# A third PSUM bank for the visits, two matmul groups in another bank, and the router's steps one place earlier

## The chip, the cores and the metric

The kernel runs on one core of a Trainium2 chip. The metric is the device time of one execution in microseconds. Three timed runs of the kernel before gave 4075.95, 4081.71 and 4083.36 us (median 4081.71). The profiled execution took 4071.0 us.

## What is computed

Two layers over a graph of 6,250 nodes with 256 features and 106,250 edges sorted by destination (self-loops included). The change lies in the second layer alone, which is, for node rows x:

```
xn  = layernorm(x)
x   = x + (xn @ W_self + mean over edges of xn[src] @ W_neigh + b) + mix(xn)
mix(xn): attn = softmax(k^T v) per head over all nodes;  y = xn + attn applied to q
         y + gelu(layernorm(y)*g + b @ w_fc1 + b_fc1) @ w_fc2 + b_fc2
h   = layernorm(x)
x   = x + shared_mlp(h) + sum over the best 2 of 4 experts of weight * expert(h)
      (weights: softmax(h @ gW + gb), top 2, softmax again; MLPs of three layers with relu)
```

All of it is in fp32.

## The kernel before, in words

Nodes stand in 49 tiles of 128 rows. The program is a row of blocks; each ends with all engines meeting. Three of the blocks are passes over the edges, and this change touches the last one (from L1813) and the short block ahead of it (L1702 to L1809).

**The short block** loads the mixer's weights by eight DMAs on SyncE's queue (L1707 to L1714), all counted on one semaphore. TensorE and VectorE then turn the Gram matrix of xn into a 256x512 weight `gws` (attention and W_self folded in), in a chain of small matmuls and copies. Its temporaries (`wqkv`, `gram`, `t1` and so on) lie in `rows`, the ring of 16 buffers that the third pass will gather edge rows into. GpSimd meanwhile sets the whole accumulator `ACC` (12544 columns) to zero (L1719), clears one temporary (L1720) and writes a constant (L1721). TensorE starts after all eight DMAs and all three of these.

**The third pass.** The sorted edges make 880 *visits* of 128 edges each. GpSimd gathers the 128 source rows of a visit into the ring by one indirect DMA (L1847), at most 16 ahead of TensorE. TensorE multiplies them with a 128x128 one-hot matrix (L1940, two instructions per visit), which ScalarE (L1858, L1862) or VectorE (L2044) has made. The product goes to half a PSUM bank, a pair of visits fills a bank, and the banks alternate between `ps[0]` and `ps[1]`: before pair n TensorE waits (L1938) until VectorE has added pair n-2. VectorE adds each half to `ACC` (L2056) once the pair is complete, and it loads the column offsets of 16 visits into registers at every sixteenth visit (L178 is the helper).

Between the visits the rest of the layer is worked off. Function `turns` (L732) writes the order by hand. Turn i has 18 or 19 visits and 18 *places* q = 0 to 17 (and a last one); at each place an engine first issues its `side(i, q)` and then one visit. In turn i the work is on four tiles: na = i+1 (attention product), b = i (the mixer's MLP), s = i-1 (residual and norm, VectorE alone), f = i-2 (experts). Every engine keeps its own program order; only semaphores tie them. What matters here, with TensorE's places first:

- q0, q1, q2: transposes for na, f and b (L1963, L1968, L1973). q3: gate logits (L1978), then the first-layer groups of the experts `first_ffn` k = 0 (L1955). q4: k = 1, 2. q5: k = 3, then a wait for `lg` (VectorE has read the gate logits, L2104), because k = 4 goes to the bank columns where they lay; then k = 4. q6: k = 5. q7: the attention product, 4 instructions of 512 columns into the whole of `ps[2]` (L1993). q8 to q10: the mixer's first layer, groups k = 0 to 5 (L1948), k = 4 and 5 into `ps[5]`. q11: second expert layers (L2006, L2008). q12: after `wg` a transpose of the gate weights (L2013). q13 to q15: the mixer's second layer (L2017), and in q14 after `wtc` the spreading of the weights (L2023). q16, q17: third expert layers (L2027, L2028, L2032).
- VectorE: `gate(f, k)`, ten tiny steps: k = 0, 1 in q4 (they end in `lg`), 2, 3 in q6, 4, 5 in q7 (they end in `pr`), 6, 7 in q8, 8, 9 in q9; `weights(f)` in q10 (ends in `wg`); the copy of the transposed weights in q13 (L2174, `wtc`). W2, the sum that reads the attention product, in q8 (L2160, `w2s`). Beside these two layer norms advance by one and two steps per place (lines 963 to 981).
- ScalarE: exp of the logits in q5, relu of the experts' groups in q6 and q7, second exp in q8 (L1905), gelu in q11 (L1910).

Of the kernel before, what the change touches and what calls it, by code (L numbers as in the profile page):

```python
# [22 lines left out]
ALU = mybir.AluOpType  # L23
# [3 lines left out]
P = 128  # L27
N = 6250
D = 256
# [76 lines left out]
def build(nc, A, out):  # L106

    with ExitStack() as ctx:
# [1574 lines left out]
        wqkv = rows[:, 0:1536].rearrange("p (c n) -> p c n", c=2)  # L1683
        gram = rows[:, 1536:2048].rearrange("p (c n) -> p c n", c=2)
        t1 = rows[:, 2048:2560].rearrange("p (c n) -> p c n", c=2)
        wq1T = rows[:, 2560:3072].rearrange("p (c n) -> p c n", c=2)
        abd = rows[:, 3072:3328].rearrange("p (c n) -> p c n", c=2)
        abT = rows[:, 3328:3584].rearrange("p (c n) -> p c n", c=2)
        bqc = rows[:, 3584:3586]
        bqm = rows[:, 3600:3728]  # L1690
        csum, nmx = rows[:, 3586:3588], rows[:, 3588:3590]
        rsm = rows[:, 3590:3592]
        nval = rows[0:1, 3592:3593]
        att = rows[:, 3728:3856].rearrange("p (c n) -> p c n", c=2)
# [7 lines left out]
        with nc.Block() as block:  # L1702
            s_w, s_v, s_p, s_a, s_z3, s_gt, s_gc = (sem("i_" + n) for n in "w v p a z gram_t gram_c".split())

            @block.sync
            def _(sp):
                sp.dma_start(wqkv, A["L1_mix_w_qkv"].rearrange("(c p) n -> p c n", p=P)).then_inc(s_w, 16)  # L1707
                sp.dma_start(bqkv, A["L1_mix_b_qkv"].rearrange("(a n) -> a n", a=1)).then_inc(s_w, 16)
                sp.dma_start(bqc, A["L1_mix_b_qkv"][0:D].rearrange("(c p) -> p c", p=P), allow_slow_non_contiguous=True).then_inc(s_w, 16)
# [5 lines left out]
                sp.wait_ge(s_w, 8 * 16)  # L1715
# [14 lines left out]
            def _(pe):  # L1730
                pe.wait_ge(s_w, 8 * 16)
                pe.wait_ge(s_z3, 3)
# [35 lines left out]
            def _(v):  # L1768
# [9 lines left out]
                link(v.tensor_copy(rows[:, 2048:2560], ps[1][:, :]))  # L1778
# [8 lines left out]
                link(v.tensor_copy(rows[:, 2560:3072], ps[4][:, :]))  # L1787
# [3 lines left out]
                v.wait_ge(s_z3, 3)  # L1791
# [6 lines left out]
                link(v.tensor_copy(rows[:, 3328:3584], ps[5][:, 0:D]))  # L1798
# [14 lines left out]
        s_gr = [sem(f"j_g{u}") for u in range(RING // 2)]  # L1813
# [8 lines left out]
        def m_f1(k):  # L1822
            return ps[4][:, k * P:(k + 1) * P] if k < 4 else ps[5][:, (k - 4) * P:(k - 3) * P]
# [4 lines left out]
        with nc.Block() as block:  # L1828
# [12 lines left out]
            @block.gpsimd  # L1841
            def _(g):
                for x in range(VIS):
                    u = x % RING
                    if x >= RING and x % 2 == 0:
                        g.wait_ge(s_mv, (x + 2 - RING) // 2)
                    g.indirect_dma_start(out=rows[:, u * D:(u + 1) * D], out_offset=None, in_=table[2],  # L1847
                                         in_offset=bass.IndirectOffsetOnAxis(ap=src_idx[:, x:x + 1], axis=0)).then_inc(s_gr[u // 2], 16)

            @block.scalar  # L1850
            def _(a):
# [18 lines left out]
                def side(i, q):  # L1870
# [26 lines left out]
                    if q == 7 and has(f):  # L1897
                        a.wait_ge(*l1.after(f))
# [3 lines left out]
                    if q == 8 and has(f):  # L1902
                        a.wait_ge(*pr.after(f))
                        a.wait_ge(*wg.room(f))
                        a.activation(x4, p4, ACT.Exp, bias=n2).then_inc(e2.sem, 1)  # L1905
# [23 lines left out]
            def _(pe):  # L1929
                start(pe, tp, gm, tn, f1, f2, ftp, gt, l1a, l1, l2, wt, bw, l3)  # L1930

                def visit(x):
# [280 lines left out]
```

## Time and profile before

| | |
|---|---|
| timed runs (3) | 4075.95, 4081.71, 4083.36 us |
| profiled execution | 4071.0 us, of it 4069.3 us from the first to the last instruction |
| short block | 2767 to 2811 us |
| third pass | 2811 to 4069 us; visits from 2819.5 to 4029.9 us |
| TensorE / VectorE / GpSimd busy, whole span | 81% / 58% / 66% |

Times inside the trace count from the first instruction. A row of the trace's order of time has its start, its length, the engine and the line, and in square brackets how long the engine sat idle before it and whose work ended that. "PEld" is TensorE's weight load, which overlaps the matmuls. Instructions in a row follow each other closer than the length of one, because matmuls are pipelined and their ends modelled: 256 columns of fp32 come every 0.215 us, 128 columns every 0.11 us.

### The profile page before, as it was taken

How to read it: one execution, taken by the hardware profiler on the slowest of the kernel's cores; microseconds unless marked ns; L12 is line 12 of the kernel's file. 1: busy time of each engine (PE TensorE's matmuls, PEld its weight loads, DVE VectorE, ACT ScalarE, POOL GpSimd, SP SyncE). 2: the span in 40 equal slices, each digit the busy share in tenths (PEclk: the TensorE clock that was granted, in tenths of full speed). 3: DMA queues.
4: the chain of work that ended last, by engine and by line, in shares of the span. 5: the costliest groups of instructions: out<-in, count | busy, mean ns of one | idle time of the engine just before them, and what ended most of it. 6: DMA issues, size and time to landing. Idle time of an engine off the chain costs nothing. (4 is left out here: it accounts for less than half of the span.)

```text
span 4069.3 us, 58095 instructions
## 1 busy us (share of the span) xinstructions
PE 3277.6 (81%) x15028; PEld 2486.5 (61%) x15028; DVE 2367.5 (58%) x8479; ACT 1846.6 (45%) x4614; POOL 2698.7 (66%) x2858
## 2 busy tenths in 40 slices
PE   7767666766666787888888888776999999999998
PEld 4544444444444465666667666664777777777777
DVE  6444444444444455666666665363777777777776
ACT  4344444444443444544445442132555555555554
POOL 4177777777776777777777773043776676666762
PEclk9677877787877788999999998886999999999999
DMA  4353333333333434666666666642333333333331
GB/s 123 95 159 111 112 110 111 110 112 110 110 112 97 118 120 141 192 194 203 200 193 197 194 193 223 201 136 75 109 104 101 101 102 102 101 101 101 103 101 48
DMA packets 268651, 532.12 MB, mean 131 GB/s; under 512 B 57942, under 2 KB 165653, under 8 KB 268199
## 3 DMA queue, kind: packets, MB, share of 16 engines
q0 software_dynamic: 139296, 386.65, 32.2%
q1 hardware_dynamic: 129030, 141.78, 11.0%
q8 instruction: 126, 2.06, 0.2%
q14 instruction: 199, 1.62, 0.1%
HBM read 463.88 MB, written 64.34 MB: 130 GB/s over the span
## 5 line engine op out<-in xcount | busy, mean ns | idle before, releaser
L1847 POOL DMA_INDIRECT rows<-table,src_idx x880 | 845.0, 960 | 388.2 <-issue 219.9
L786 POOL DMA_INDIRECT rows<-table,src_idx x880 | 835.3, 949 | 268.1 <-issue 265.4
L1061 POOL DMA_INDIRECT rows<-table,src_idx x880 | 835.2, 949 | 267.9 <-issue 253.5
L880 DVE TENSOR_TENSOR AR<-AR,ps 128x256 f32 x880 | 370.6, 421 | 592.3 <-PE ps L837 529.1
L1224 DVE TENSOR_TENSOR AR<-AR,ps 128x256 f32 x880 | 370.1, 421 | 329.1 <-PE ps L1135 244.4
L1940 PE MATMUL ps<-rows,AR 128*128 128x256 f32 x1760 | 538.6, 392 | 7.9 <-issue 3.6
L2056 DVE TENSOR_TENSOR AR<-AR,ps 128x256 f32 x880 | 369.2, 420 | 177.2 <-PE ps L1940 101.6
L837 PE MATMUL ps<-rows,work 128*128 128x256 f32 x880 | 315.0, 486 | 172.9 <-DMA rows<-table,src_idx 151.7
L1135 PE MATMUL ps<-rows,work 128*128 128x256 f32 x1168 | 362.6, 419 | 74.4 <-DMA rows<-table,src_idx 64.9
L837 PEld LDWEIGHTS ps<-rows,work 128*128 128x128 f32 x880 | 188.0, 238 | 272.2 <-issue 141.9
L1940 PEld LDWEIGHTS ps<-rows,AR 128*128 128x128 f32 x1760 | 285.8, 193 | 72.0 <-issue 50.3
L1135 PEld LDWEIGHTS ps<-rows,work 128*128 128x128 f32 x1168 | 221.5, 208 | 151.6 <-issue 105.0
L797 ACT ACTIVATE work<-iota,dst_rel 128x128 f32<-128x128 f32 x440 | 140.5, 390 | 231.7 <-PE ps L837 231.4
L837 PE MATMUL ps<-rows,mring 128*128 128x256 f32 x440 | 163.8, 501 | 100.5 <-DMA rows<-table,src_idx 92.5
L1135 PE MATMUL ps<-rows,mring 128*128 128x256 f32 x592 | 186.7, 420 | 72.0 <-DMA rows<-table,src_idx 66.0
L1176 PE MATMUL ps<-wreg,work 128*128 128x512 f32 x392 | 209.3, 662 | 30.1 <-DVE work L1328 15.2
L1111 ACT ACTIVATE AR<-AR 128x1024 f32<-128x1024 f32 x49 | 51.8, 1057 | 393.9 <-DVE AR L1341 393.9
L837 PE MATMUL ps<-rows,gates 128*128 128x256 f32 x440 | 163.6, 500 | 83.1 <-DMA rows<-table,src_idx 67.7
L1092 ACT ACTIVATE work<-iota,dst_rel 128x128 f32<-128x128 f32 x584 | 185.8, 391 | 84.1 <-PE ps L1135 84.1
L1955 PE MATMUL ps<-AR 128*128 128x128 f32 x1176 | 176.0, 282 | 22.5 <-DVEq L2104 21.6
L837 PEld LDWEIGHTS ps<-rows,mring 128*128 128x128 f32 x440 | 97.3, 245 | 153.7 <-issue 79.6
L1955 PEld LDWEIGHTS ps<-AR 128*128 128x128 f32 x1176 | 159.9, 191 | 37.2 <-DVEq L2104 29.0
(508 smaller groups left out, 6687.0 us busy)
## 6 DMA issues: line engine op xcount, KB each, us to landing
AR<-in_L_ffn_Wd SPq DMA_DIRECT2D x48, 1024.0 KB, 7.2
rows<-table,src_idx POOLq DMA_INDIRECT x2640, 2.8
AR<-h_sorted SPq DMA_DIRECT2D x52, 512.0 KB, 3.9
table<-AR SPq DMA_DIRECT2D x147, 128.0 KB, 2.2
AR<-in_x SPq DMA_DIRECT2D x4, 1536.0 KB
out_x<-XN SPq DMA_DIRECT2D x48, 128.0 KB
AR<-in_L_ffn_bd SPq DMA_DIRECT2D x40, 128.0 KB, 8.3
y_sorted<-AR SPq DMA_DIRECT2D x40, 128.0 KB
```

Source lines behind the costliest of these rows:

```text
L786: g.indirect_dma_start(out=rows[:, u * D:(u + 1) * D], out_offset=None, in_=table[0], in_offset=bass.IndirectOffsetOnAxis(ap=src_idx[:, x: ...
L837: ins = pe.matmul(pair(x), hot[Q % 4][:, x % 4 * P:(x % 4 + 1) * P], rows[:, x % RING * D:(x % RING + 1) * D], start=True, stop=True)
L880: v.tensor_tensor(acc, acc, pair(y), ALU.add).then_inc(s_av, 1)
L1061: g.indirect_dma_start(out=rows[:, u * D:(u + 1) * D], out_offset=None, in_=table[1], in_offset=bass.IndirectOffsetOnAxis(ap=src_idx[:, x: ...
L1092: ins = a.activation(hot[Q % 3][:, k * P:(k + 1) * P], iota[:, :], ACT.Abs, scale=-1.0, bias=dst_rel[:, 4 * Q + k:4 * Q + k + 1])
L1135: ins = pe.matmul(pair(x), hot[Q % 3][:, x % 4 * P:(x % 4 + 1) * P], rows[:, x % RING * D:(x % RING + 1) * D], start=True, stop=True)
L1176: ins = pe.matmul(ps[3 + h][:, :], f_xT[:, c * P:(c + 1) * P], ff1[:, c, h * 512:(h + 1) * 512], start=c == 0, stop=c == 1)
L1224: v.tensor_tensor(acc, acc, pair(y), ALU.add).then_inc(s_av, 1)
L1847: g.indirect_dma_start(out=rows[:, u * D:(u + 1) * D], out_offset=None, in_=table[2], in_offset=bass.IndirectOffsetOnAxis(ap=src_idx[:, x: ...
L1940: ins = pe.matmul(ps[x // 2 % 2][:, x % 2 * D:(x % 2 + 1) * D], hot[Q % 4][:, x % 4 * P:(x % 4 + 1) * P], rows[:, u * D:(u + 1) * D], star ...
L1955: ins = pe.matmul(f_l1(k), w, f_xT[:, c * P:(c + 1) * P], start=c == 0, stop=c == 1)
L2056: v.tensor_tensor(acc, acc, ps[x // 2 % 2][:, y % 2 * D:(y % 2 + 1) * D], ALU.add).then_inc(s_av, 1)
```

## The change

- The third pass's visits use three banks, `ps[0]`, `ps[1]`, `ps[5]`: TensorE waits for the adds of pair n-3.
- The mixer's groups k = 4 and 5 go to `ps[2]`, after the attention product of the next tile has been read there. So TensorE waits for `w2s` ahead of q10, and ahead of q0's transposes for the gelu of the previous tile.
- TensorE: the attention product moves from q7 to q5; `first_ffn` k = 4 (with the wait for `lg`) from q5 to q6, k = 5 from q6 to q7; the transpose of the gate weights (with the wait for `wg`) from q12 to q11.
- VectorE: gate steps 4, 5 to q6; 6, 7 to q7; 8, 9 to q8; `weights` to q9; W2 to q7; the copy L2174 to q12.
- ScalarE: the second exp (behind `pr`) moves to q7, the last two relus to q8.
- In the short block the temporaries lie in `ACC` and no longer in the ring. GpSimd clears one temporary, writes the constant, issues the first 16 gathers and clears columns 3856 to 12544 of `ACC`. VectorE clears columns 0 to 3856 as its first instruction of the pass and waits for it. The first three weight DMAs have a semaphore of their own, and TensorE waits for these three and two GpSimd instructions only.

```
-        wqkv = rows[:, 0:1536].rearrange("p (c n) -> p c n", c=2)
+        wqkv = ACC[:, 0:1536].rearrange("p (c n) -> p c n", c=2)
...
             def _(g):
-                g.memset(ACC, 0.0).then_inc(s_z3, 1)
-                g.memset(rows[:, 3072:3328], 0.0).then_inc(s_z3, 1)
+                g.memset(ACC[:, 3072:3328], 0.0).then_inc(s_z3, 1)
                 g.memset(nval, float(N)).then_inc(s_z3, 1)
+                for x in range(RING):
+                    gather3(g, x)
+                g.memset(ACC[:, ATMP:T * D], 0.0).then_inc(s_z3, 1)
...
-                pe.wait_ge(s_w, 8 * 16)
-                pe.wait_ge(s_z3, 3)
+                pe.wait_ge(s_wq, 3 * 16)
+                pe.wait_ge(s_z3, 2)
...
-            return ps[4][:, k * P:(k + 1) * P] if k < 4 else ps[5][:, (k - 4) * P:(k - 3) * P]
+            return ps[4][:, k * P:(k + 1) * P] if k < 4 else ps[2][:, (k - 4) * P:(k - 3) * P]
+
+        banks = [0, 1, 5]
...                                                             # ScalarE
                     if q == 7 and has(f):
+                        a.wait_ge(*pr.after(f))
+                        a.wait_ge(*wg.room(f))
+                        a.activation(x4, p4, ACT.Exp, bias=n2).then_inc(e2.sem, 1)
+                    if q == 8 and has(f):
                         a.wait_ge(*l1.after(f))
                         for k in range(4, 6):
...
-                    if q == 8 and has(f):
-                        a.wait_ge(*pr.after(f))
...                                                             # TensorE
-                        if x >= 4:
-                            pe.wait_ge(s_av, x - 2)
+                        if x >= 2 * len(banks):
+                            pe.wait_ge(s_av, x + 2 - 2 * len(banks))
...
                         pe.wait_ge(*w2s.room(na))
+                        if na > 1:
+                            pe.wait_ge(s_gl, 6 * (na - 1))
...
                         first_ffn(f, (3,)).then_inc(l1a.sem, 1)
+                    if q == 6 and has(f):
                         pe.wait_ge(*lg.after(f))
                         first_ffn(f, (4,))
-                    if q == 6 and has(f):
+                    if q == 7 and has(f):
                         first_ffn(f, (5,)).then_inc(l1.sem, 1)
-                    if q == 7 and has(na):
+                    if q == 5 and has(na):
                         pe.wait_ge(*xt.after(na))
...
+                    if q == 10 and has(na) and has(b):
+                        pe.wait_ge(*w2s.after(na))
...
                         ins.then_inc(l2.sem, 1)
-                    if q == 12 and has(f):
                         pe.wait_ge(*wg.after(f))
...                                                             # VectorE
+                v.memset(ACC[:, 0:ATMP], 0.0).then_inc(s_az, 1)
+                v.wait_ge(s_az, 1)
...
                     if q == 6 and has(f):
-                        gate(f, 2)
-                        gate(f, 3)
-                    if q == 7 and has(f):
-                        gate(f, 4)
-                        gate(f, 5)
-                    if q in (8, 9) and has(f):
-                        gate(f, 2 * q - 10)
-                        gate(f, 2 * q - 9)
-                    if q == 10 and has(f):
+                        for k in range(2, 6):
+                            gate(f, k)
+                    if q in (7, 8) and has(f):
+                        gate(f, 2 * q - 8)
+                        gate(f, 2 * q - 7)
+                    if q == 9 and has(f):
                         weights(f)
-                    if q == 8 and has(na):
+                    if q == 7 and has(na):
                         v.wait_ge(*gm.after(na))
...
-                    if q == 13 and has(f):
+                    if q == 12 and has(f):
                         v.wait_ge(*wt.after(f))
```

## Rows read from the trace of the kernel before

**Rows 1.** Busy time by stretch: us, then PE, PEld, DVE, ACT, POOL busy (instructions), PEclk, DMA.
```profile
2871.00:2899.00 28.00, 25.56 (x138) 20.58 (x138) 19.19 (x74) 13.79 (x38) 21.29 (x23) 0.94 0.38 109
3214.00:3315.00 101.00, 94.14 (x542) 78.08 (x542) 74.04 (x293) 54.30 (x141) 69.16 (x74) 1.00 0.35 101
```

**Rows 2.** Order of time, TensorE: the attention product of turns 10 and 43.
```profile
3076.25 1.88 PE L1993 MATMUL ps<-AR 128*128 128x512 f32 x4
...
3908.99 1.88 PE L1993 MATMUL ps<-AR 128*128 128x512 f32 x4
```

**Rows 3.** Whom TensorE waited for, 3076 to 4022 us: total, times, longest.
```profile
PE ps L2023 <- DVE AR L2174: 29.8, 35, 1.5
PE ps L1955 <- DVEq L2104: 16.9, 29, 1.1
PE ps L2013 <- DVEq L2137: 4.8, 10, 0.5
```

**Rows 4.** The same for VectorE, its largest row.
```profile
DVE AR L2056 <- PE ps L1940: 78.1, 108, 2.5
```

**Rows 5.** The page's costliest groups: busy us, mean ns, idle before.
```profile
L1847 POOL DMA_INDIRECT rows<-table,src_idx x880 | 845.0, 960 | 388.2 <-issue 219.9
...
L1061 POOL DMA_INDIRECT rows<-table,src_idx x880 | 835.2, 949 | 267.9 <-issue 253.5
```

**Rows 6.** Order of time, TensorE, one turn from product to product.
```profile
3101.87 1.88 PE L1993 MATMUL ps<-AR 128*128 128x512 f32 x4
...
3109.99 0.27 PE L2013 MATMUL ps<-ident,AR 128*5 128x128 f32 x1
...
3113.62 0.71 PE L2023 MATMUL ps<-AR 5*128 5x128 f32 x4 [0.70 <-DVE AR L2174]
...
3124.80 0.71 PE L1955 MATMUL ps<-AR 128*128 128x128 f32 x4 [0.52 <-DVEq L2104]
...
3126.66 1.88 PE L1993 MATMUL ps<-AR 128*128 128x512 f32 x4
```

**Rows 7.** Order of time, VectorE, from the pair of places 4, 5 to the copy.
```profile
3126.18 0.97 DVE L2056 TENSOR_TENSOR AR<-AR,ps 128x256 f32 x2
...
3129.11 0.97 DVE L2056 TENSOR_TENSOR AR<-AR,ps 128x256 f32 x2 [0.97 <-PE ps L1940]
...
3130.44 0.68 DVE L2160 TENSOR_TENSOR AR<-ps,AR 128x512 f32<-128x512 f32 x1
...
3137.90 0.27 DVE L2174 COPY AR<-ps 5x128 f32<-5x128 f32 x1
```

**Rows 8.** Order of time, TensorE, a turn whose first visit is odd.
```profile
3175.45 0.71 PE L1955 MATMUL ps<-AR 128*128 128x128 f32 x4 [1.05 <-DVEq L2104]
...
3189.11 0.71 PE L2023 MATMUL ps<-AR 5*128 5x128 f32 x4 [1.05 <-DVE AR L2174]
```

**Rows 9.** Order of time, the short block's start.
```profile
2767.32 10.55 POOL L1719 MEMSET AR<- 128x12544 f32 x1 [33.15 <-POOLq L1538]
...
2771.72 0.62 SPq L1714 DMA_DIRECT2D wreg<-in_L_mix_b_fc  x1
...
2778.24 0.45 PE L1734 MATMUL ps<-ident,rows 128*128 128x128 f32 x1 [13.69 <-POOL rows L1721]
```

**Rows 10.** Order of time, the pass's start: W2's first sum, the first visits.
```profile
2818.17 0.69 DVE L2160 TENSOR_TENSOR AR<-ps,AR 128x512 f32<-128x512 f32 x1 [6.02 <-PE ps L1993]
...
2819.46 1.06 PE L1940 MATMUL ps<-rows,AR 128*128 128x256 f32 x2
```

**Rows 11.** Order of time, TensorE: its long waits before visits, turns 0 and 1.
```profile
2843.35 0.87 PE L1940 MATMUL ps<-rows,AR 128*128 128x256 f32 x2 [2.29 <-issue]
...
2865.01 0.67 PE L1940 MATMUL ps<-rows,AR 128*128 128x256 f32 x2 [2.38 <-DVE AR L2056]
```

**Rows 12.** The gathers of the pass: length ns, first and last start us.
```profile
L1847 POOL DMA_INDIRECT rows<-table,src_idx x880: 940/946/1525, 2811.2 to 4010.4; - x176
```

More of the change, by code:

```diff
@@ L1680, in _, with gather3 @@
                         v.sem_inc(s_nf, 1)
-        wqkv = rows[:, 0:1536].rearrange("p (c n) -> p c n", c=2)
[L1684 to L1694, printed above, removed]
+        s_gr = [sem(f"j_g{u}") for u in range(RING // 2)]
+        ATMP = 3856
+        def gather3(g, x):
+            u = x % RING
+            g.indirect_dma_start(out=rows[:, u * D:(u + 1) * D], out_offset=None, in_=table[2],
+                                 in_offset=bass.IndirectOffsetOnAxis(ap=src_idx[:, x:x + 1], axis=0)).then_inc(s_gr[u // 2], 16)
+        wqkv = ACC[:, 0:1536].rearrange("p (c n) -> p c n", c=2)
+        gram = ACC[:, 1536:2048].rearrange("p (c n) -> p c n", c=2)
+        t1 = ACC[:, 2048:2560].rearrange("p (c n) -> p c n", c=2)
+        wq1T = ACC[:, 2560:3072].rearrange("p (c n) -> p c n", c=2)
+        abd = ACC[:, 3072:3328].rearrange("p (c n) -> p c n", c=2)
+        abT = ACC[:, 3328:3584].rearrange("p (c n) -> p c n", c=2)
+        bqc = ACC[:, 3584:3586]
+        bqm = ACC[:, 3600:3728]
+        csum, nmx = ACC[:, 3586:3588], ACC[:, 3588:3590]
+        rsm = ACC[:, 3590:3592]
+        nval = ACC[0:1, 3592:3593]
+        att = ACC[:, 3728:3856].rearrange("p (c n) -> p c n", c=2)
         bqkv = work[0:1, 0:768]
@@ L1777, in _ @@
                 v.wait_ge(s_p, 5)
-                link(v.tensor_copy(rows[:, 2048:2560], ps[1][:, :]))
+                link(v.tensor_copy(ACC[:, 2048:2560], ps[1][:, :]))
                 link(v.tensor_copy(t2row, ps[2][0:1, 0:D]))
@@ L1786, in _ @@
                 v.wait_ge(s_p, 8)
-                link(v.tensor_copy(rows[:, 2560:3072], ps[4][:, :]))
+                link(v.tensor_copy(ACC[:, 2560:3072], ps[4][:, :]))
                 v.wait_ge(s_a, 2)
@@ L1797, in _ @@
                 v.wait_ge(s_p, 10)
-                link(v.tensor_copy(rows[:, 3328:3584], ps[5][:, 0:D]))
+                link(v.tensor_copy(ACC[:, 3328:3584], ps[5][:, 0:D]))
                 v.wait_ge(s_p, 14)
@@ L1809, in _ @@
                 link(v.tensor_tensor(gws[:, :, D:2 * D], gws[:, :, D:2 * D], gws[:, :, 0:D], ALU.add))
-        s_gr = [sem(f"j_g{u}") for u in range(RING // 2)]
+        s_az = sem("j_acc_zero")
         s_mv, s_av, s_abs, s_hota, s_hotv = (sem("j_" + n) for n in "visit added abs hot_a hot_v".split())
@@ L1842, in _ @@
             def _(g):
-                for x in range(VIS):
-                    u = x % RING
-                    if x >= RING and x % 2 == 0:
+                for x in range(RING, VIS):
+                    if x % 2 == 0:
                         g.wait_ge(s_mv, (x + 2 - RING) // 2)
-                    g.indirect_dma_start(out=rows[:, u * D:(u + 1) * D], out_offset=None, in_=table[2],
-                                         in_offset=bass.IndirectOffsetOnAxis(ap=src_idx[:, x:x + 1], axis=0)).then_inc(s_gr[u // 2], 16)
+                    gather3(g, x)
             @block.scalar
@@ L1936, in visit @@
                     if x % 2 == 0:
-                        if x >= 4:
-                            pe.wait_ge(s_av, x - 2)
+                        if x >= 2 * len(banks):
+                            pe.wait_ge(s_av, x + 2 - 2 * len(banks))
                         pe.wait_ge(s_gr[u // 2], x // RING * 32 + 32)
-                    ins = pe.matmul(ps[x // 2 % 2][:, x % 2 * D:(x % 2 + 1) * D], hot[Q % 4][:, x % 4 * P:(x % 4 + 1) * P],
+                    ins = pe.matmul(pair(x), hot[Q % 4][:, x % 4 * P:(x % 4 + 1) * P],
                                     rows[:, u * D:(u + 1) * D], start=True, stop=True)
@@ L2055, in visit @@
                                 v.wait_ge(s_av, y)
-                            v.tensor_tensor(acc, acc, ps[x // 2 % 2][:, y % 2 * D:(y % 2 + 1) * D], ALU.add).then_inc(s_av, 1)
+                            v.tensor_tensor(acc, acc, pair(y), ALU.add).then_inc(s_av, 1)
                     if x % 8 == 4 and x // 4 + 2 < VIS // 4:
```

16 lines of the change are left out of this document (8 added, 8 removed).

## The prediction

> **What bounds the kernel now.** I read the clock and the busy time by stretch first. In the steady part of the third pass TensorE has its full clock (1.00) and is busy 94.14 of 101 us, while VectorE has 74.04 and GpSimd 69.16 [rows 1]. That is not yet a bound: the places where TensorE stops are what the change can reach. From the attention product of turn 10 to that of turn 43 there are 33 turns in 832.74 us, so 25.23 us a turn [rows 2]. The reader is to see three columns that all come out near 23 us.
>
> TensorE: the turn between two attention products took 24.79 us [rows 6]. In it the engine stood 0.70 us before L2023 and 0.52 us before L1955. Both idle times are counted from a modelled end that lies about 0.17 us behind the point where the next matmul could have followed, so they are 0.87 and 0.70 us of the turn, and L2013 comes 0.23 us late without an idle mark. 24.79 - 1.80 = 23.0 us is what TensorE needs for 18 visits (23.1 with the extra visit of each third turn).
>
> VectorE: over 3076 to 4022 us (37.5 turns) it waited 78.1 us for a visit [rows 4], 2.1 us a turn. Its own work, register loads included, is 25.2 - 2.1 = 23.1 us a turn.
>
> GpSimd: a gather takes 0.960 us and 0.305 us until the next one (219.9 us over 721 of them) [rows 5], and a turn has 18.33, which gives 23.2 us.
>
> So no engine fills the turn. The missing 2 us are two hand-overs from VectorE to TensorE, and the ones back. TensorE waited 29.8 us for the copy of the gate weights, 16.9 us for the logits' reading and 4.8 us for the weights [rows 3], 51.5 us or 1.4 us a turn by the marks, 1.9 us with the hidden part. For a free visit bank it waits only in turns 0 and 1 [rows 11]. The third bank alone takes away nothing in a steady turn as it is; it is of use once TensorE runs further ahead of VectorE.
>
> **The change part by part, against the profiled execution of 4071.0 us** (span 4069.3 us, 1.7 us around it; it is 10.7 us below the median of the three runs, which I add at the end).
>
> *The wait for the logits (q5 to q6).* With the attention product (4 x 0.43 = 1.72 us) and one visit (0.43 us) ahead of it, TensorE comes 2.15 us later to this wait. The longest one in the steady part was 1.1 us [rows 3]; it goes, and a slack of at least 1 us is left. The product needs the tile's transposed rows, which ScalarE had ready since q1. Gain 0.5 to 0.7 us a turn for TensorE. What is late next: VectorE takes visits in pairs, and where a turn's first visit is even, the pair of places 4 and 5 is complete only behind the product.
>
> *The copy (q13 to q12) and the transpose ahead of it (q12 to q11).* I follow the even turn of [rows 6, 7]. Today's order has VectorE at the pair of places 4, 5 at 3126.18 and at the copy at 3137.90, 11.72 us later, of which 0.97 us is a wait for the visit behind the product in q7. In the new order TensorE does not stop at 3124.10: product to 3125.82, visit to 3126.25, and the pair can be added from 3126.5. VectorE's work up to the copy is the same (four gate steps, W2, the weights change places within it), without the 0.97 us of waiting and without one place's norm steps (two of some 0.17 us), so the copy starts at 3126.5 + 11.72 - 0.97 - 0.33 = 3136.9 and is done, with its semaphore, near 3137.3. TensorE, no longer held at the logits, wants it at 3136.3. It still waits 1.0 us, but 0.9 us earlier than now: the turn would be 23.9 us. In this turn the register load for 16 visits (1.3 us) fell before the pair; in some 8 of 18 positions it falls inside the stretch and lengthens it, 0.6 us on average. Even turns: 24.5 us.
>
> In an odd turn [rows 8] the pairs are 5, 6 and 7, 8. The product stands ahead of visit 5 with another place before the pair is due, so VectorE loses nothing there. Both waits of 1.05 us are there today; the first goes whole, the second mostly: by the same count VectorE's copy comes 2.0 us earlier. Odd turns: 23.7 to 23.8 us, held up by VectorE's own 23.1 us. Odd and even come in runs of three, half of the turns each: 24.1 us a turn, 1.13 us less than now. There are 45 such turns (2 to 46): 51 us.
>
> *New waits.* TensorE waits for W2 ahead of q10. Behind it are the mixer's last two groups, all of the experts' second layer and every later visit. Counted from q0, TensorE is at q10 at 11.45 us with nothing in its way. VectorE ends W2, by the lengths in [rows 7] and behind six gate steps, at about 10.7 us, with a one-hot matrix (0.69 us) ahead of it at 11.3 us, with the register load as well at 12.0 us or more. So it is free in most turns and costs 0.5 to 1 us in a few; I put 0.1 us a turn, inside the 24.1. The bounds are 0 and 1.2 us. The wait for the gelu at q0 is for work that TensorE itself has already waited for in q13 to q15: nothing, both ways. The transpose in q11 waits for weights that VectorE now makes in q9; both moved by one place, nothing (bounds -0.2 to 0.3 us a turn, by L2013's row [rows 3]).
>
> *ScalarE.* The second exp is ahead of the last relus now. Both are short (0.30 us and 0.63 us), the exp needs `pr` one place earlier and gets it, and their readers (VectorE's q9, TensorE's q11) come 2 us and more later. Nothing.
>
> *The third bank.* It removes 2.29 and 2.38 us before visits in turns 0 and 1 [rows 11]; I take 4.5 us. In the even turn above the pair of places 12, 13 would find two banks' adds not done by some 0.5 us, so the third bank also keeps the 24.1.
>
> *The short block.* TensorE starts at 2778.24 us, released by GpSimd's third instruction, which stood behind the 10.55 us clearing [rows 9]. The eight DMAs had all been issued by 2772.3, and the traffic ended near the same time, so the three that count now, one third of the bytes and first in the queue, set the start: about 2774 to 2775. Gain 3.5 us, bounds 0 (the gathers' 2 MB share the engines) and 9. The 16 gathers and the smaller clearing end near 2796, under a chain that ends near 2810. The ring is full when the pass begins, but the first visits are released by W2's sum at 2818.17 [rows 10], so no visit comes earlier by it.
>
> *VectorE's clearing of 3856 columns.* No row shows it. GpSimd clears 0.84 ns a column [rows 9], so 3.2 us; VectorE's 512-column sum takes 0.68 us [rows 7], so 5.1 us at the most. VectorE stands idle for 6.02 us before its first W2 [rows 10], and the one-hot matrix behind the clearing is wanted at the fifth visit. Nothing; without that cover it would be 5.1 us once.
>
> Sum: 51 + 4.5 + 3.5 = 59 us. 4071.0 - 59 = 4012 us, and 4012 + 10.7 = 4022.7, so 4022 us for the median.
>
> **A rule weighed.** The mean gather of this pass takes 0.960 us against 0.949 us in the pass before, with single ones up to 1.525 us [rows 5, 12]. The Trainium skill, "SBUF — State Buffer", section "Who interferes with whom", says that VectorE instructions with two SBUF inputs, or in a two-port mode, and GpSimd hold up one another through a shared port pair. By that rule the gathers lengthen as VectorE's work is packed closer, and GpSimd would become the bound first. The rows' 11 ns make 0.2 us a turn, and that trace agrees in kind only; if every gather took as much as 1.1 us, a turn would be 25.8 us and nothing would be gained.
>
> **The rivals.**
>
> (a) *All three stalls go and nothing takes their place*: the turn is 23.2 us, by GpSimd. For it: three engines need 23.0 to 23.2 us and the third bank loosens them. Against it: VectorE and TensorE hand over in both directions several times a turn, and my even turn still stops. 45 x 2.03 = 91 us and 8 us: 3972, as a median 3983 us. Chance 0.12.
>
> (b) *The stall only moves behind the product.* VectorE is late at q5's visit in even turns and the 1.3 us load and the one-hots weigh fully: turn 24.9 us, 15 + 8 = 23 us gained, 4059 us. For it: the loop from the visit in q5 over VectorE to the copy and back is 10.7 us + 12.8 us + hand-overs before loads. Chance 0.22.
>
> (c) *The change doesn't do what it says*: the moves of both engines cancel each other and only the 8 us at the start remain: 4074 us. Chance 0.09.
>
> (d) *Slower: the wait for W2 at q10.* It becomes the stall of every turn, at 1.2 us (12.6 us against 11.45 us), and the wait for the copy stays at 1.0 us because VectorE is no earlier: 23.1 + 1.2 + 1.0 + 0.3 = 25.6 us. 45 x 0.4 = 18 us more, 8 us less: 4092 us. It decides where VectorE's W2 ends later than 11.45 + 1.3 us in the ordinary turn. Against it: W2 stands one place earlier than now. Chance 0.12.
>
> **How the numbers follow.** My forecast has a chance of 0.45. Cases (a), (b) and the forecast are faster by over 0.2% (8 us, about what this kernel's measurement can tell from none): 0.79, of which I give 0.01 to "same" for (b)'s upper edge. (c) lies at that bound. Faster 0.78, same 0.10, slower 0.12. The range goes from (a) at 3982 to (c) at 4074 us.
>
> **What would show it.** Right: TensorE's wait for L2104 gone, the one for L2174 at under 20 us over 33 turns, a distance of 23.9 to 24.3 us between attention products, VectorE's waits for L1940 under 1.5 us a turn, TensorE's first matmul of the short block before 2775 us. Wrong: a row "PE L1948 <- DVE L2160" of more than 0.3 us a turn, GpSimd without any wait for TensorE (then it is the bound), or odd turns no shorter than even ones.

## The result, and the profile after

The changed kernel takes 4042.4 us (median of 4 runs, 4033.62 to 4048.94); the kernel before took 4078.8 us in the runs beside it (4069.96 to 4083.36). The ratio is 0.9912, 95% interval 0.9886 to 0.9938: faster by 36 us. The direction and the range held; the gain was 36 us by these medians and 37 us by the profiled executions, where 59 were forecast. The profiled execution took 4033.62 us (span 4031.9) against 4071.0 before (span 4069.3).

The first two passes are the same code in both kernels, and yet the short block ahead of the third pass starts at anything from 2760 to 2777 us in the profiles of this study. So I compare one thing throughout: the time from GpSimd's first clearing of the short block to the end of the span, called the **last stretch** below. Before it was 4069.3 - 2767.3 = 1302.0 us [rows 9], after it is 4031.9 - 2767.2 = 1264.7 us.

Busy time by stretch, the changed kernel (us; PE, PEld, DVE, ACT, POOL busy (instructions); PEclk; DMA share; GB/s). The first two rows answer to [rows 1]:

```profile
2871.00:2899.00 28.00, 26.51 (x161) 22.22 (x160) 21.11 (x83) 16.40 (x45) 21.26 (x23) 1.00 0.38 109
3214.00:3315.00 101.00, 95.33 (x559) 80.06 (x559) 76.78 (x300) 55.62 (x148) 73.12 (x76) 1.00 0.36 105
3086.60:3114.82 28.22, 26.56 (x137) 21.28 (x136) 18.56 (x74) 14.23 (x39) 17.63 (x19) 0.88 0.31 89
3114.82:3140.17 25.35, 23.72 (x140) 19.72 (x139) 18.94 (x77) 13.73 (x36) 18.08 (x20) 1.00 0.36 106
3100.00:3110.00 10.00, 8.96 (x27) 6.38 (x28) 5.21 (x22) 0.00 (x0) 3.79 (x4) 0.66 0.23 67
```

Where the clock is whole, the engines do 2 to 5% more instructions than before in the same 101 us. The third and fourth row are two turns that follow one another, from product to product. In the first TensorE's granted clock is 0.88, so it had its lower level, 1.2 GHz, for a part of the turn; the last row shows where. In those ten microseconds it ran only 27 matmuls and still counts as 90% busy.

The attention product of turns 10 and 43, as [rows 2]: 33 turns in 815.21 us, 24.70 us a turn where it was 25.23. From turn 3 to turn 46 it was 25.32 us before (even 25.27, odd 25.38) and is 24.63 us after (even 25.52, odd 23.74).

```profile
3060.55 1.88 PE L2008 MATMUL ps<-AR 128*128 128x512 f32 x4
...
3875.76 1.88 PE L2008 MATMUL ps<-AR 128*128 128x512 f32 x4
```

Whom TensorE waited for, 3076 to 3986 us, as [rows 3] (total, times, longest). The waits for the logits and for the weights are gone; the one for the copy has fewer turns and longer ones, 1.05 us each where it was 0.85:

```profile
PE ps L2039 <- DVE AR L2189: 28.3, 27, 2.0
PE ps L1992 <- ACT AR L1891: 4.1, 5, 0.9
PE ps L1987 <- DVE XN L2198: 0.5, 2, 0.3
```

The same for VectorE, as [rows 4]. The second row is new: the sum of the tile into the norm's input finds its semaphore late, because the weights are now made directly ahead of it.

```profile
DVE AR L2074 <- PE ps L1952: 44.0, 52, 2.5
DVE XN L2180 <- DVE AR L2153: 25.0, 37, 0.7
```

The page's groups for the gathers of the third and second pass, as [rows 5]. The third pass's are 12 ns longer than the second's; before it was 11:

```profile
L1688 POOL DMA_INDIRECT rows<-table,src_idx x880 | 847.2, 963 | 352.9 <-issue 241.0
...
L1061 POOL DMA_INDIRECT rows<-table,src_idx x880 | 836.8, 951 | 268.0 <-issue 250.8
```

Order of time, TensorE, from one attention product to the next in an even turn (turn 11, 28.22 us), as [rows 6]:

```profile
3086.60 1.88 PE L2008 MATMUL ps<-AR 128*128 128x512 f32 x4
...
3088.75 0.61 PE L1967 MATMUL ps<-AR 128*128 128x128 f32 x4
...
3096.22 0.27 PE L2029 MATMUL ps<-ident,AR 128*5 128x128 f32 x1
...
3098.49 1.03 PE L2033 MATMUL ps<-wreg,AR 128*128 128x256 f32 x4
3101.04 0.71 PE L2039 MATMUL ps<-AR 5*128 5x128 f32 x4 [1.52 <-DVE AR L2189]
...
3104.19 1.06 PE L2043 MATMUL ps<-AR 128*128 128x256 f32 x2
...
3107.35 1.91 PE L2048 MATMUL ps<-AR 128*128 128x256 f32 x4
...
3114.82 1.88 PE L2008 MATMUL ps<-AR 128*128 128x512 f32 x4
```

The reader is to see two things. There is one marked wait, 1.52 us, at the spreading, and none at 3088.75 (L1967, the group behind the logits' wait) or at 3096.22 (L2029, the transpose of the gate weights), where before the turn could break. And behind it the lengths double: four matmuls of 256 columns take 1.91 us at 3107.35 and 1.03 us at 3098.49. That is the half clock of the window 3100:3110. A turn whose mean granted clock is below 0.98 is called **throttled** below: the changed kernel has nine of them between turns 3 and 46, all even, with clocks of 0.88 to 0.94 and lengths of 26.05 to 28.62 us. The kernel before has one, turn 45.

VectorE in the same turn, as [rows 7]: it waits 1.11 us for the visit behind the product, 1.28 us in the register load, 0.68 us for the weights, and then comes to the copy.

```profile
3089.05 0.97 DVE L2074 TENSOR_TENSOR AR<-AR,ps 128x256 f32 x2 [1.11 <-PE ps L1952]
...
3092.22 0.15 DVE L973 TENSOR_SCALAR gsml<-gsml 128x1 int32<-128x1 int32 x1 [1.28 <-issue]
...
3095.98 0.42 DVE L2180 TENSOR_TENSOR XN<-XN,AR 128x256 f32 x1 [0.68 <-DVE AR L2153]
...
3100.71 0.27 DVE L2189 COPY AR<-ps 5x128 f32<-5x128 f32 x1
```

The short block and the first turn, in order of time, as [rows 9, 10]:

```profile
2772.57 0.48 PE L1745 MATMUL ps<-ident,AR 128*128 128x128 f32 x1 [8.12 <-DMA AR<-in_L_mix_b_qkv]
...
2787.69 7.36 POOL L1732 MEMSET AR<- 128x8688 f32 x1
...
2792.73 2.36 DVE L1796 TENSOR_SCALAR AR<-AR 128x2 f32<-128x2 f32 x1
...
2808.84 3.27 DVE L2055 MEMSET AR<- 128x3856 f32 x1 [2.31 <-issue]
2810.90 3.78 PE L2008 MATMUL ps<-AR 128*128 128x512 f32 x4 [1.05 <-ACT AR L1887]
...
2814.72 0.69 DVE L2175 TENSOR_TENSOR AR<-ps,AR 128x512 f32<-128x512 f32 x1 [1.88 <-PE ps L2008]
...
2816.02 1.92 PE L1952 MATMUL ps<-rows,AR 128*128 128x256 f32 x4
```

Counted from the first clearing, TensorE starts 5.6 us earlier and the first product comes only 3.4 us earlier, because a scaling of 128 x 2 numbers takes 2.36 us and ends as GpSimd's clearing ends.

**Where the 37 us came from**: the block up to the first product 3.4 us; from that product to turn 0's 13.12 before and 11.94 after, 1.2 us; turns 0 and 1 together 43.55 and 42.03, 1.5 us; turn 2 27.37 and 24.92, 2.4 us; turns 3 to 46 44 x 0.69 = 30.4 us. From turn 47's product to the end it is 56.68 and 58.29, 1.6 us lost again. That makes the 37.3 us of the last stretch.

### The profile page after: what moved, and what is told of

It reads as the page before. It is cut to its first block and busy times, and to the rows that moved or that the text cites. A ratio compares the mean times of both kernels' runs of the same rounds, so it can differ in the third digit from the quotient of the medians.

```text
span 4031.9 us, 58097 instructions
## 1 busy us (share of the span) xinstructions
PE 3284.1 (81%) x15028; PEld 2510.8 (62%) x15028; DVE 2370.3 (59%) x8480; ACT 1844.1 (46%) x4614; POOL 2702.3 (67%) x2858
## 5 line engine op out<-in xcount | busy, mean ns | idle before, releaser
L837 PE MATMUL ps<-rows,work 128*128 128x256 f32 x880 | 330.9, 507 | 165.4 <-DMA rows<-table,src_idx 152.6
L1135 PE MATMUL ps<-rows,work 128*128 128x256 f32 x1168 | 367.6, 424 | 85.8 <-DMA rows<-table,src_idx 77.4
L837 PEld LDWEIGHTS ps<-rows,work 128*128 128x128 f32 x880 | 198.3, 250 | 267.3 <-issue 143.5
L1135 PEld LDWEIGHTS ps<-rows,work 128*128 128x128 f32 x1168 | 223.2, 210 | 163.3 <-issue 105.6
L1158 PE MATMUL ps<-AR 128*128 128x256 f32 x640 | 177.3, 406 | 9.9 <-DMA AR<-in_L_ffn_bd 9.9
L837 PEld LDWEIGHTS ps<-rows,gates 128*128 128x128 f32 x440 | 95.5, 239 | 137.4 <-issue 70.9
```

The lines of the kernel that those rows point to most:

```text
L837: ins = pe.matmul(pair(x), hot[Q % 4][:, x % 4 * P:(x % 4 + 1) * P], rows[:, x % RING * D:(x % RING + 1) * D], start=True, stop=True)
L1135: ins = pe.matmul(pair(x), hot[Q % 3][:, x % 4 * P:(x % 4 + 1) * P], rows[:, x % RING * D:(x % RING + 1) * D], start=True, stop=True)
L1158: ins = pe.matmul(ps[6][:, 0:D], XHT[:, k * P:(k + 1) * P], XW[b % 2][:, k * D:(k + 1) * D], start=k == 0, stop=k == HC - 1)
```

## The experiments

All are edits of the changed kernel except the eighth. In the table "even" and "odd" are mean distances between attention products in turns 3 to 46 by the parity of the turn's first visit; "throttled" counts the throttled turns among these; ratios are against the kernel before in the same session.

| Kernel | median us | ratio (95%) | last stretch us | even | odd | throttled |
|---|---|---|---|---|---|---|
| before | 4078.8 | 1 | 1302.0 | 25.27 | 25.38 | 1 |
| changed | 4042.4 | 0.9912 (0.9886 to 0.9938) | 1264.7 | 25.52 | 23.74 | 9 |
| changed, once more | 4045.0 | 0.9933 (0.9917 to 0.9950) | 1265.0 | 25.51 | 23.77 | 9 |
| filler | 4023.9 | 0.9888 (0.9872 to 0.9905) | 1251.5 | 24.80 | 23.73 | 0 |
| two banks | 4025.9 | 0.9890 (0.9873 to 0.9906) | 1255.9 | 24.97 | 23.89 | 0 |
| two banks, once more | 4029.4 | 0.9884 (0.9867 to 0.9900) | 1256.3 | 24.98 | 23.91 | 0 |
| product by parity | 4000.1 | 0.9830 (0.9813 to 0.9846) | 1224.0 | 23.52 | 23.88 | 0 |
| the same, two banks | 3995.1 | 0.9800 (0.9783 to 0.9816) | 1230.3 | 23.65 | 24.06 | 0 |
| spreading late | 4009.0 | 0.9856 (0.9839 to 0.9872) | 1237.3 | 24.23 | 23.82 | 1 |
| short block only | 4070.2 | 0.9986 (0.9977 to 0.9996) | 1298.1 | 25.25 | 25.42 | 1 |
| clearing first | 4041.7 | 0.9926 (0.9902 to 0.9949) | 1264.8 | 25.52 | 23.75 | 9 |
| load first | 4019.0 | 0.9871 (0.9853 to 0.9890) | 1240.4 | 24.71 | 23.48 | 3 |
| all four | 3977.2 | 0.9768 (0.9752 to 0.9784) | 1208.4 | 23.14 | 23.63 | 0 |
| all four, two banks | 3984.3 | 0.9786 (0.9770 to 0.9803) | 1214.7 | 23.32 | 23.76 | 0 |

The kernel and its repetition differ by 0.3 us in the last stretch, two banks and its repetition by 0.4 us: by these two pairs the measure tells differences of 1 us, which the medians can't. It comes from the one profiled execution of each kernel.

**Filler: is it the half clock?** Three matmuls that nobody reads, ahead of the wait in even turns:

```
                     if q == 14 and has(f):
+                        if bound(i) % 2 == 0:
+                            for _ in range(3):
+                                pe.matmul(ps[4][:, 0:D], ident[:, :], fc2[:, 0, :], start=True, stop=True)
                         pe.wait_ge(*wtc.after(f))
```

> The changed kernel, and in turns whose first visit is even TensorE does three matmuls of 256 columns into a free part of ps[4] (three times 0.43 us) just ahead of its wait for the copy of the gate weights; their result is never read. Theory A (TensorE's idle time of 1.35 us and more before the spreading is what is followed by the half clock in 9 even turns, at 2.5 us each): the idle time shrinks below 0.8 us, no steady stretch shows less than 0.99 of the clock, the even turns go from a mean of 25.5 to 24.5 to 24.8 us, and the kernel gains 12 to 20 us on the changed one, 4042 to about 4026 us. Rival B (the slow stretches come by themselves, or from the copy's lateness itself): they stay, the fillers cost a little where the wait is shorter than 1.3 us, 4042 to 4050 us.

The last stretch is 13.2 us shorter, by work added to TensorE. TensorE's clock and its wait, the first row to be held beside 3010:3110 of the changed kernel, which has PEclk 0.95 and 529 matmuls:

```profile
3010.00:3110.00 100.00, 98.14 (x568) 81.85 (x567) 76.23 (x296) 54.74 (x143) 72.70 (x75) 1.00 0.37 104
```
```profile
PE ps L2042 <- DVE AR L2192: 6.9, 17, 1.0
```

No turn is throttled any more, and even turns fell from 25.52 to 24.80, as theory A has it. The filler costs its own time too, so the loss by the clock is larger than these 0.72 us a turn. In the changed kernel the 13 even turns at full clock took 24.49 us and the 9 throttled ones 27.02, 2.53 us more, 22.8 us together. Not all of that is the clock, because the throttled turns also had the longer waits at the spreading, 1.64 us in the mean against 1.06. Two counts give the clock's part. With the filler the same nine turns took 24.99 us, 2.03 us less each (18.3 us together), and the other 13 took 24.66, 0.17 us more. And each throttled turn's length times the missing share of its mean granted clock, summed over the nine, gives an estimate of 18.8 us.

**Two banks: what is the third bank worth?**

```
-        banks = [0, 1, 5]
+        banks = [0, 1]
```

> The changed kernel with ps[0] and ps[1] alone for the visits; everything else as changed. Theory A (as predicted: the third bank keeps TensorE from waiting for the adds in turns 0 and 1, 4.5 us, and by about 0.5 us in each of 22 even turns): 10 to 16 us slower than the changed kernel, 4055 us, with rows in which TensorE waits for L2074 before a visit. Rival B (TensorE did not wait for a bank in any steady turn before, so the bank is worth only the start): 4 us, 4046 us. Rival C (the bank is what made the change faster at all): back to 4078 us.

> The changed kernel with two visit banks once more, beside it. Theory A (with two banks TensorE's lateness in even turns is the same 1 to 2 us but in several short waits, after none of which the clock is halved; with three it is one long wait that in 9 turns is followed by 2.5 us of half clock): 5 to 15 us faster than the changed kernel. Rival B (the earlier figure was the other chip's): 5 to 10 us slower than the changed kernel, by the 0.5 us of the even turns.

> The changed kernel once more, to stand beside the next three on one chip. Both theories: 0.990 to 0.993 of the kernel before.

Shorter by 8.8 us and 8.7 us in the last stretch (15.5 us by the medians of the repetition, where both were timed side by side): here the third bank costs time, which none of the first three expectations had. Whom TensorE waited for with two banks, 3076 to 3986 us:

```profile
PE ps L1952 <- issue: 13.3, 18, 1.6
PE ps L1952 <- DVE AR L2074: 9.6, 12, 1.3
PE ps L1992 <- ACT AR L1891: 4.4, 6, 0.9
PE ps L2039 <- DVE AR L2189: 4.3, 10, 0.7
```

TensorE waits as long in all (27.2 us before visits and at the spreading against 28.3), but most of it stands ahead of visits and not ahead of the spreading, and no turn falls to half clock. In most turns this also cuts the wait into shorter pieces. Not in all: five turns have a single wait of 1.44 to 1.60 us before a visit, and the clock stays whole behind it. The longest, in turn 24:

```profile
3413.85 0.67 PE L1952 MATMUL ps<-rows,AR 128*128 128x256 f32 x2 [1.60 <-issue]
```

At the start the bank gains and loses: with three banks turn 0 took 18.54 us and turn 1 23.49 at a clock of 0.88, with two 20.64 and 20.83, turn 1 at 1.00. The window where they part, three banks and two banks:

```profile
2860.00:2870.00 10.00, 10.00 (x54) 8.61 (x53) 6.33 (x25) 7.05 (x17) 7.56 (x9) 0.83 0.35 105
```
```profile
2860.00:2870.00 10.00, 9.38 (x57) 7.75 (x58) 7.53 (x28) 6.82 (x17) 7.56 (x9) 1.00 0.37 104
```

**The product's place by parity: is VectorE late because of the product?**

```
+                    if q == (5 if bound(i) % 2 else 6) and has(na):
                         pe.wait_ge(*xt.after(na))
...
-                    if q == 5 and has(na):
```

> The changed kernel with the attention product in place 6 instead of 5 in turns whose first visit is even, so that it never stands between the two visits of VectorE's next pair. Theory A (in even turns VectorE is made late by the product ahead of the pair of places 4 and 5, and that is why the copy is late): VectorE's wait for the visit there goes, the wait before the spreading falls from 1.3 us to below 0.7 us in even turns, the half clock goes with it, even turns 25.5 to about 24.0 us; 22 x 1.5 = 33 us, 4042 to about 4010 us. Rival B (VectorE's own work up to the copy is the length, wherever the product stands): even turns stay within 0.3 us of 25.5, 4036 to 4046 us.

Even turns fell by 2.0 us to 23.52, and odd ones took 0.14 us more. TensorE's wait for the copy in this kernel, and VectorE's wait for a visit, which had been 44.0 us:

```profile
PE ps L2039 <- DVE AR L2189: 11.2, 23, 1.0
```
```profile
DVE AR L2074 <- PE ps L1952: 9.3, 23, 0.9
```

So the 1.11 us for which VectorE waited behind the product was the first cause of the late copy, and the late copy that of the throttled turns. In the last stretch this is 40.7 us for a move of four matmuls by one place in half of the turns, more than the whole change had brought.

With two banks on top:

> Two visit banks, and the attention product in place 6 in even turns. Theory A (the bank buys slack between TensorE and VectorE and is worth most once the even turn's stall is gone): waits for L2074 before visits come back at 0.3 to 0.8 us a turn, 15 to 30 us slower than three banks with the same product, 4015 to 4030 us. Rival B (the stall came from the product's place alone; with that right two banks do): within 5 us of 4000 us.

The expectation was 15 to 30 us slower with two banks; the median is 5 us lower, the last stretch 6.3 us longer. The two medians come from different sessions, and in the profiled executions (3993.51 and 3993.65 us in all) the short block starts at 2761.6 us here and at 2767.9 with three banks, so I go by the stretch: once no turn behind the first ones is throttled, the third bank is worth 6 us, a fifth to two fifths of what was expected of it.

**Spreading late:** its place moved from q14 to q15, behind the two groups of the mixer's second layer in that place; everything else as in the changed kernel.

```
-                    if q == 14 and has(f):
+                    if q == 15 and has(f):
                         pe.wait_ge(*wtc.after(f))
```

> The changed kernel with the spreading of the gate weights (and its wait for the copy) behind the second-layer groups of place 15 instead of in place 14, 1.3 us of matmuls later. Theory A (TensorE only asks too early; nothing else hangs on the copy): the wait goes below 0.2 us a turn, the half clock goes too, even turns near 24.0 us, 4042 to 4008 us. Rival B (the wait moves on: VectorE's product L2193 is later and TensorE stands before the third layer in place 17): the half clock goes, but a new wait of 0.3 to 0.8 us a turn stands before that place, 4020 to 4030 us.

```profile
PE ps L1987 <- DVE XN L2198: 6.5, 19, 0.9
PE ps L2039 <- DVE AR L2189: 3.4, 9, 0.7
```

27.4 us less in the last stretch. The wait for the copy went from 28.3 to 3.4 us and 6.0 us came up at the next place that needs VectorE, the transposes of the norm (L1987), 0.2 us a turn. One turn, the 30th, is still throttled. Only the reader was moved here, not the cause.

**Short block only:** the kernel before with the short block's part of the change (temporaries in `ACC`, 16 gathers at once, VectorE's clearing) and nothing else.

> The kernel before with only the short block changed: temporaries in ACC, the split weight semaphore, the 16 gathers ahead, VectorE's clearing of 3856 columns in the pass. The pass keeps its two banks and its order. Theory A: the block ends 3.4 us earlier as in the changed kernel (5.7 us at its start, 2.2 us given back where VectorE stands beside GpSimd's clearing), and the pass's turns are as before: 3 to 5 us faster than the kernel before. Rival B (the gathers ahead also shorten the first turns): 8 us or more.

3.9 us in the last stretch, 5.7 us by the ratio (interval 1.6 to 9.4 us), as theory A has it; the waits of TensorE stand as in [rows 3]:

```profile
PE ps L2033 <- DVE AR L2186: 29.7, 35, 1.5
PE ps L1965 <- DVEq L2116: 16.0, 28, 1.1
```

**Clearing first:** GpSimd clears `ACC` before it issues the 16 gathers.

```
+                g.memset(ACC[:, ATMP:T * D], 0.0).then_inc(s_z3, 1)
                 for x in range(RING):
                     gather3(g, x)
-                g.memset(ACC[:, ATMP:T * D], 0.0).then_inc(s_z3, 1)
```

> The changed kernel with GpSimd's clearing of the sums ahead of its first sixteen gathers instead of behind them. Theory A (a shared port: in the changed kernel the scaling of 128x2 at L1796 took 2.36 us instead of 0.17 and ended inside GpSimd's clearing of 2787.69 to 2795.05): with the clearing done near 2775 this instruction is back at 0.17 us and the block ends about 2.2 us earlier, the first attention product near 2808.7 instead of 2810.9. Rival B (the instruction was late for another reason, a releaser that the profile doesn't name): it keeps its 2.36 us, and the product stays near 2810.9. In either case it is a one-off of 2 us in 4030, not to be seen in the time; the answer is in the rows.

```profile
2777.42 0.31 POOL L1728 MEMSET AR<- 128x256 f32 x1 [33.15 <-POOLq L1538]
...
2777.70 7.35 POOL L1730 MEMSET AR<- 128x8688 f32 x1
...
2803.28 0.39 DVE L1796 TENSOR_SCALAR AR<-AR 128x2 f32<-128x2 f32 x1
...
2819.48 3.76 PE L2008 MATMUL ps<-AR 128*128 128x512 f32 x4 [1.05 <-ACT AR L1887]
```

The scaling takes 0.39 us (0.18 in the kernel with all four edits, which has the same order), and the product comes 42.06 us after the first clearing instead of 43.69. So theory A's cause holds, with 1.6 us for its 2.2. The 1.6 us were there and were lost again: turns 0 and 1 took 0.2 and 1.5 us more. Ahead of turn 0 TensorE stood 2.96 us for the norm instead of 1.86, and turn 0's product took 2.85 us at 2831.39 where it had been 1.92, partly at half clock.

**Load first:** the five weight steps behind the sum into the norm's input, still in place 9.

```
-                    if q == 9 and has(f):
-                        weights(f)
...
                         v.tensor_tensor(x, x, W2[:, D:2 * D], ALU.add).then_inc(s_xa, 1)
+                    if q == 9 and has(f):
+                        weights(f)
```

> The changed kernel with VectorE's weights (five small steps) behind the sum of the tile into the norm's input in place 9, instead of ahead of it. Theory A: the changed kernel's 25.6 us of waits of that sum for the weights' semaphore (38 waits of 0.7 us over 37 turns), where before it was 14.6 us for the register load, are paid by TensorE in the half of turns that wait for the copy of the gate weights: 0.3 us a turn there, 5 to 8 us in all, and where the wait at the spreading falls under 1.35 us fewer stretches of half clock follow, up to 10 us more: 4020 to 4035 us where the changed kernel has 4040 to 4045. Rival B: VectorE's gap is filled by its later wait for a visit in the even turns (53 waits of 2.5 us at most), so nothing moves: within 4 us of the changed kernel. Rival C: the weights come later to TensorE's transpose in place 11, which then waits 0.3 us a turn: 5 to 10 us slower than the changed kernel.

24.3 us in the last stretch, three times the expectation's first part and more than both of its parts together. VectorE's waits in this kernel (its row for the weights' semaphore, 25.0 us, is gone, and 3.7 us of the register load stand in its place), then TensorE's:

```profile
DVE AR L2074 <- PE ps L1952: 36.2, 53, 2.5
...
DVE XN L2178 <- issue: 3.7, 13, 0.3
```
```profile
PE ps L2039 <- DVE AR L2189: 19.5, 22, 1.8
```

Odd turns gain 0.26 us, even ones 0.81, since 6 of 9 throttled turns went too. By the count of clock shares the clock cost 18.8 us before this edit and 6.8 us after it, so about half of the 24.3 us came by way of the clock. That the edit had cost anything I had not seen: the weights and the sum are neighbours in place 9 only since the change.

**All four**, three and two banks:

> Four edits of the changed kernel together, three banks: the attention product in place 6 in turns whose first visit is even and in place 5 in the others; the spreading behind the third layer's first groups in place 15; GpSimd's clearing ahead of its first gathers; the weights behind the sum in place 9. Theory A (each takes away a different wait): the product's place gave 23.52 us in even turns and 23.88 in odd ones, with 10.8 us of waits left at the spreading; the later spreading takes away most of those, 5 to 8 us; 2 us from the clearing, a few from the weights: 3985 to 3993 us. Rival B (GpSimd's 952 ns and 0.3 us a gather are the bound, 23.2 us a turn, and most of the gain was already there with the product's place): 3995 to 4002 us, within 5 us of the product's place alone.

> The same four edits with the visits in two banks, as in the kernel before. Theory A (the third bank is worth nothing here, as with the product's place alone, where two banks gave 3995 us and three 4000): within 5 us of the kernel with three banks. Rival B (once the spreading is late too, TensorE is ahead of VectorE by more than two banks hold): 10 us or more slower than with three banks, in waits before visits that name the adds at L2074.

3977 us, the fastest version, 2.3% under the kernel before where the change has 0.9%. Neither number was met: the time lies 8 us under the range of theory A (3985 to 3993), and two banks are 6.3 us longer in the last stretch, 7 us by the medians, between theory A's 5 and rival B's 10; the ratios' intervals just overlap. What is left of waiting in it: busy time of 3214:3315 and TensorE's longest row, with three banks.

```profile
3214.00:3315.00 101.00, 99.99 (x587) 84.25 (x588) 79.45 (x311) 57.59 (x152) 76.08 (x80) 1.00 0.38 110
```
```profile
PE ps L1992 <- ACT AR L1891: 5.0, 7, 0.9
```

TensorE stands at 99.99 of 101 us, and even turns take 23.14 us, the 23.0 to 23.1 that the prediction counted as its own work.

## Why the prediction was right, and where not

- **The logits' wait goes, with the product ahead of it: right.** It has no row any more.
- **Odd turns 23.7 to 23.8 us: right**, 23.74.
- **Even turns 24.5 us: right for 13 of 22, which took 24.49, and wrong for the nine throttled ones, 27.02.** This is the step that failed. I had the mechanism (the pair of places 4 and 5 is complete only behind the product, and the copy is late by it) and priced the wait that is left at its own length. It was 1.30 us in the mean instead of 1.0, and behind nine of them TensorE's granted clock fell to its lower level for a few microseconds, which was in no term of the sum. The filler took these falls away. By the estimate above they cost 18.8 us. The sum had 51 us for turns 2 to 46, and these turns gave 32.8: the 18.2 us that are missing are about what the clock took. That it comes out so closely is partly luck: without the clock's loss turns 3 to 46 would be near 24.2 us and not 24.1, and the kernel before had 25.32 us there and not the 25.23 the sum started from, some 4 us each way.
- **The signs named beforehand: three of five.** No wait for the logits, visits that VectorE waits 1.2 us a turn for (39.6 us over the 33 turns), and a first matmul of the short block at 2772.57 us came as said. TensorE's wait for the copy was 26.1 us over 33 turns instead of under 20, and the products stood 24.70 us apart instead of 23.9 to 24.3. None of the signs of being wrong was there.
- **Why a total of the waits did not show it.** In [rows 3] the waits summed to 51.5 us and one turn of 44 was throttled; now the three rows above sum to 32.9 us and nine are throttled. Twelve of the 22 even turns have a wait of 1.35 us or more at the spreading; the nine throttled ones are among them, and none with less is throttled. But such a wait in one piece is neither sufficient nor necessary. Turns 17, 18 and 24 waited 1.39, 1.52 and 1.47 us and stayed at full clock, and so did turns 23, 30 and 37 of the kernel with the load first (1.83, 1.73 and 1.55 us), turns 9 and 16 of the kernel before (1.53 and 1.55 us) and the five turns with two banks. With the spreading late there was a throttled turn, the 30th (25.20 us, clock 0.93), behind a wait of only 0.47 us. Shown is that the falls go when the idle time ahead of the spreading is filled or taken away; what decides in which turns they come stays open.
- **The place of the weights, "moved by one place, nothing": wrong.** The sum of the tile now comes directly behind the weights, and VectorE waits 0.68 us 37 times where it waited 0.38 us for the register load. I take it that the load no longer overlaps the weights; no row shows this by itself. Undone, it was worth 24 us, about half of which went by way of the clock.
- **The third bank, 4.5 us in turns 0 and 1 and a help later: wrong in sign as the kernel stands.** Turns 0 and 1 gave 1.5 us, and with two banks they would have given 2.1. Over the pass it costs 8.8 us: with it TensorE's waiting moves from the visits to the spreading and nine turns are throttled, with two banks none. With the product moved it brings 6.3.
- **New wait for W2, 0.1 us a turn: small, as said**, one marked wait of 0.26 us, and by the starts five turns late by 0.2 to 0.4 us, 1.4 us in all; so rival (d), the slower one, had nothing under it. (c) is out by the lines of the odd turns. (a), 23.2 us a turn, needed the copy's wait gone; it is near what all four further edits reach (23.38 us a turn). (b), the stall moving behind the product at 24.9 us a turn, is the one that came half true: the stall did move there, the mean turn was 24.63, and much of its price came from the clock.
- **The short block, 3.5 us: right in size, 3.4, as two errors.** The start came at 2772.6 us, earlier than my 2774 to 2775, and 2.2 us were given back at L1796. I had looked for what the later clearing delays in the chain of semaphores only, not at what runs beside it. The Trainium skill, "SBUF — State Buffer", section "Who interferes with whom", has `tensor_scalar` among the instructions that can take the port pair shared with GpSimd when their operands allow it, and says that whoever comes second is blocked for the whole of the other's instruction. The rows agree: the scaling ended at 2795.09 us, the clearing at 2795.05, and it was short when the clearing stood elsewhere.
- **VectorE's clearing, 3.2 to 5.1 us, hidden: right**, 3.27 us, with VectorE still waiting 1.88 us behind it.
- **The gathers would not be the bound: right.** They got 3 ns longer in the third pass and 2 ns in the second, which the change does not touch.

## What to carry to other kernels

When a change takes some of several waits of the fullest engine away, look at the one that is left, not only at the sum: waiting at one place can cost the TensorE clock on top of itself, here 18.8 us beside 28.3 us of waits, and a buffer that lets the engine run ahead to that place can make it worse (8.8 us). Which waits the clock falls behind can't be told from their length here; read the granted clock turn by turn. First ask who is late and why; moving the four matmuls that a pair waits behind brought 40.7 us, as much as the change itself. And where the parts of a program ahead of the change vary by several microseconds from run to run, compare from a fixed instruction on, not by totals.

## What was not expected of the hardware

- Single idle times of TensorE of 1.35 to 1.97 us before the spreading went with a fall of the granted clock nine times of twelve (0.66 in the mean of 10 us, 3100 to 3110). Such a turn was 2.5 us longer than the other even ones in the mean, some 2.1 us of it by the clock, and up to 4.1 us (turn 25, 28.62 us). With two banks as much idle time, most of it before visits and in single waits of up to 1.60 us, went with no fall in 44 turns.
- The falls are of the program, not of chance: the changed kernel, its repetition and the kernel with the clearing first had them in the same nine turns, with lengths within 0.1 us.
- VectorE clears 128 x 3856 in 3.27 us, 0.85 ns a column, the same pace as GpSimd's (8688 columns in 7.36 us).
- A VectorE instruction on 128 x 2 numbers took 2.36 us instead of 0.17 beside a clearing by GpSimd; a 128 x 512 comparison of two operands (L2062) kept a median of 0.68 us over 110 times beside the gathers.
